# Last attention: where the two maximum tiles of a step stand between its scores and its value product

## The chip, the cores and the metric

One core of a Trainium2 chip. The metric is the device time of one execution in microseconds (us). TensorE (PE in the rows) does the matmuls, VectorE (DVE) and ScalarE (ACT) read their results out of PSUM, GpSimd (POOL) does small elementwise work, and SyncE (SP) issues the DMAs. Each engine runs its own list of instructions in order, and they meet at semaphores.

## The reference

Two gated layers over `x` of 4 batches x 1024 tokens x 256 channels: cross attention, a feed-forward mixture, cross attention again, and at the end a self attention in place of the second feed-forward. Only the last one matters here:

```python
qkv = (x @ W_qkv).reshape(Bx, Nx, 3, H, D)            # 16 heads of 16
...
pos = sim > 0.9
logits = jnp.einsum('bqhd,bkhd->bhqk', q * scale, k)
def masked_attn(tok_mask):
    ...
    a = jax.nn.softmax(l, axis=-1)
    return jnp.einsum('bhqk,bkhd->bqhd', a, v)
```

Each token attends within its own class (positive or negative), and the first five, the registers, to both.

## The kernel before

The last attention is cut into 16 units (`UNITS`), each 4 heads of one batch. A unit has 16 steps `s`: two halves of 512 queries, and in each half 8 blocks of 128 keys. A step makes, for its 4 heads, the scores of 128 keys by 512 queries, their exponentials, and the product with the values. Softmax needs each query's maximum before the scores are exponentiated: it is found one unit ahead, from a cheaper form of the scores, and enters the real scores as one more row of the contraction (row 98, `MAX_ROW`).

TensorE's list in the steady part is `body_pe`. Its pieces are:

- `scores2(u, s, h, j)`, L1607 to L1614: the scores of one head, four matmuls of 99 rows x 32 columns x 512 (L1612), one for each 32 keys, side by side on the four column groups. The result goes to one of three PSUM banks, 4 to 6, taken in turn (`take_third`, in the order of the list `USERS`). Score n can be written only once the user three places before it has been read.
- `values2(u, s, j)`, L1597 to L1605: the value product of one step, float32, four matmuls of 128 rows x 32 columns x 512 which the trace shows as two passes of four (L1603).
- `max_tile(p, a, j)`, L1584 to L1592: a maximum tile, two matmuls of 50 rows x 128 columns x 512 (L1590), on rows 0 and 64 of the array. It takes a pair of banks, 0 and 1 or 2 and 3, by turns (`take_pair`): tile p waits until VectorE has reduced tile p - 2 (`s_tfree`).
- `max_rows(o, half)`, L1594: a transpose (L1595) of the maxima of 16 tiles, into one of the three small banks.

In the code a step issues scores 0, 1 and 2, the value product of the step before, score 3, and then `turns(plan[2n])` and `turns(plan[2n + 1])`, which are its two maximum tiles. I call them A and B. `PLAN` holds one tile per slot, and in slots 2 and 18 the transposition (`("rows", ...)`) ahead of the tile. So one step in eight has a transposition, between score 3 and tile A. Units 0 to 14 have tiles: 15 x 16 = 240 steps with two tiles, 30 of them with a transposition. Unit 15 has none (`PLAN_LAST` keeps one transposition), and parts of the final projection take their place.

VectorE reduces each tile over 1024 columns (L2140, `reduce_tile`) and negates the transposed rows into `mro` (L2144, `rows_turn`), in the order of `PLAN` (`body_dve`). ScalarE exponentiates the scores of each step from the small banks to SBUF (L1083, `exps`); twice a unit it copies bank 7 of finished outputs out (L1090), ahead of its fourth exponential of that step. SyncE writes `mro` to DRAM and reads it back as the row 98 of the queries (`store_row`, L644 to L649), and loads the operands of units ahead. Its row for half 1 is read from step 8 of the same unit on, and the one for half 0 from step 0 of the next unit.

Of the kernel before, what the change touches and what calls it, by code (L numbers as in the profile page):

```python
# [38 lines left out]
def build_program(nc, ins, out):  # L39
    ctx = ExitStack()  # L40
    with ctx:
# [26 lines left out]
        def bank(i, n=1):  # L68
            return ps[:, 512 * i:512 * (i + n)]
# [372 lines left out]


        PLAN = [[("tile", n)] for n in range(32)]
        PLAN[2].insert(0, ("rows", 1))
        PLAN[18].insert(0, ("rows", 0))
        PLAN_LAST = [[] for _ in range(32)]
        PLAN_LAST[2].append(("rows", 1))
        PAIRS0 = 33
        TURNS = sum(len(x) for x in PLAN)  # L450

# [3 lines left out]
        def small_turn(u, what, arg):  # L455
            return 2 * u + SMALL.index((what, arg))
# [656 lines left out]
        def _(pe):  # L1113
# [54 lines left out]
            for b in range(B):  # L1168
# [5 lines left out]
                for g in range(4):  # L1174
                    n = 4 * b + g
# [401 lines left out]
            def take_third(what, n):  # L1577
                place = PLACE[what, n]
                if place >= 3:
                    before, i = USERS[place - 3]  # L1580
                    pe.wait_ge(s_sfree if before == "score" else s_bfree, i + 1)
                return third_bank(what, n)

            def max_tile(p, a, j):  # L1584

                pl = take_pair(p)
                q, h = a // 4, a % 4
                for i in range(2):
                    v = slice(64 * i, 64 * i + MROWS)
                    mm = pe.matmul(pl[:, 512 * i:512 * i + 512], QMH[j][h][v, P * q:P * q + P], KM[j][v, h, :],  # L1590
                                   start=True, stop=True)
                mm.then_inc(s_turn, 1)  # L1592

            def max_rows(o, half):  # L1594
                pe.transpose(o[0:16, 0:P], MX[:, half].rearrange("p j q -> p (j q)"), identF[:, :]).then_inc(s_turn, 1)  # L1595

            def values2(u, s, j):  # L1597
                half, k = s // 8, s % 8
                pe.wait_ge(s_sfree, 64 * u + 4 * s + 4)
                if k == 0:  # L1600
                    pe.wait_ge(s_oe2, 2 * u + half + 1)
                for h in range(4):
                    mm = pe.matmul(bank(7)[32 * h:32 * h + 32, :], VST[j][:, k, h, :], PR[:, s % 2, h, :],  # L1603
                                   start=(k == 0), stop=(k == TB - 1))
                mm.then_inc(s_pv2, 1)  # L1605

            def scores2(u, s, h, j):  # L1607
                n = 4 * s + h
                o = take_third("score", 64 * u + n)
                for c in range(4):  # L1610
                    t = P * (s % 8) + 32 * c
                    mm = pe.matmul(o[32 * c:32 * c + 32, :], KST[j][0:MAX_ROW + 1, h, t:t + 32],  # L1612
                                   QST[j][0:MAX_ROW + 1, h, 512 * (s // 8):512 * (s // 8) + 512],
                                   start=True, stop=True)  # L1614
                mm.then_inc(s_sco, 1)

            def body_pe(u, j, loads, last=False):
                jn = 1 - j
                p = PAIRS0 + 32 * u

                def turns(entries):
                    for what, arg in entries:
                        if what == "tile":
                            max_tile(p + arg, arg, jn)
                        else:
                            o = take_third("small", small_turn(u, what, arg))
                            pe.wait_ge(s_tfree, p + 16 * (1 - arg))
                            max_rows(o, arg)

                if not last:  # L1630
                    pe.wait_ge(s_mst[jn], 16 * MSTACK_DMAS * loads)
                plan = PLAN_LAST if last else PLAN
                for n, s in enumerate(ORDER):

                    us, js = (u, j) if s >= SHIFT else (u + 1, jn)
                    if s < SHIFT and last:
                        break
                    if s == 8:
                        pe.wait_ge(s_row[1], 16 * (u + 1))
                    if s == 0:  # L1640
                        pe.wait_ge(s_stk[jn], 16 * STACK2_DMAS * loads)
                        pe.wait_ge(s_row[0], 16 * (u + 2))
                    for h in range(3):
                        scores2(us, s, h, js)
                    if s == 0:
                        values2(u, 15, j)
                    else:
                        if s == 1:
                            pe.wait_ge(s_vst, u + 2)
                        values2(us, s - 1, js)  # L1650
                    scores2(us, s, 3, js)
                    turns(plan[2 * n])
                    turns(plan[2 * n + 1])
                    if last:
                        project2(n)
                if last:
                    values2(u, 15, j)

            def project2(i):
                c, q = i // 4, i % 4  # L1660
                n = NC + c
                if i == 0:
                    pe.wait_ge(s_tfree, PAIRS0 + 32 * (UNITS - 1))
                    pe.wait_ge(s_avg, 2)
                if i == 4 * (NC - 2):
                    pe.wait_ge(s_avg, 4)
                if i == 4 * (NC - 1):
                    pe.wait_ge(s_nd2, UNITS)
                if q == 0 and c >= 2:
                    pe.wait_ge(s_x3, n - 1)  # L1670
                o = bank(2 * (c % 2) + q // 2)[:, C * (q % 2):C * (q % 2) + C]
                for j in range(2):
                    mm = pe.matmul(o, OT2[:, j, c // 2, 512 * (c % 2) + P * q:512 * (c % 2) + P * q + P],  # L1673
                                   wproj[:, j, :], start=(q % 2 == 0 and j == 0), stop=(j == 1),
                                   skip_group_check=True)
                if q == 3:
                    mm.then_inc(s_wo, 1)
# [3 lines left out]
            n = 0  # L1681
# [31 lines left out]
            for u in range(UNITS):  # L1713
                body_pe(u, u % 2, (u + 1) // 2 + 1, last=u + 1 == UNITS)
# [542 lines left out]
```

## Time and profile before

| | us |
|---|---|
| median of 3 runs | 1285.85 (1282.24 to 1290.98) |
| the profiled execution | 1284.64 |
| its span, first to last instruction | 1282.9 |
| PE, DVE, ACT busy in the span | 1183.9, 985.4, 827.1 |

The span leaves out 1.7 us of the profiled execution. A row of the timeline merges neighbouring instructions of one line on one engine: its start is that of the first, its second number is the time from there to the end of the last. In the rows PE is a matmul and PEld a load of its weights, which may run beside an earlier matmul. The end of a matmul is modelled, and it runs past the start of the next: so the distance between two starts says what a matmul costs, not its length.

### The profile page before, as it was taken

Reading aid. Unit: us, or ns where it says so; the run is one execution under the profiler, and the core shown is the slowest. Engines: PE = TensorE matmul, PEld = TensorE weight load, DVE = VectorE, ACT = ScalarE, POOL = GpSimd, SP = SyncE. Lnnn points to the kernel's source line nnn. Section 1 sums busy time; section 2 is a strip of 40 time slices with the busy share of each in tenths; the row PEclk is TensorE's granted clock in tenths of the full one; section 3 lists DMA queues with packets and bytes.
Section 4 is the critical chain, followed back from the end, with each engine's and each line's share of the span. In section 5 each row is a group of like instructions: output and inputs, shape, how many; then the busy total and the mean of one; then the engine's idle time right before and its main releaser. Section 6 shows DMA issues by size and latency. Waiting matters only on the chain.

```text
span 1282.9 us, 26149 instructions
## 1 busy us (share of the span) xinstructions
PE 1183.9 (92%) x10378; PEld 543.5 (42%) x10378; DVE 985.4 (77%) x1446; ACT 827.1 (64%) x1476; POOL 247.9 (19%) x192
## 2 busy tenths in 40 slices
PE   4888992999999899987999999999999999999997
PEld 3566772555548446443332323233232332323345
DVE  4895597565545757657999999999999999999912
ACT  1224583677762463212888888888888888888872
POOL 2130224455661332370000000000000000000000
PEclk8879995999999999988999999999999999999999
DMA  6100016666520143453154534554345443554014
GB/s 196 27 1 15 2 25 113 118 131 113 104 51 1 50 147 111 142 75 52 45 99 82 74 86 77 95 93 80 80 88 93 82 84 76 99 94 80 11 41 137
DMA packets 89961, 101.73 MB, mean 79 GB/s; under 512 B 22122, under 2 KB 60268, under 8 KB 89840
## 3 DMA queue, kind: packets, MB, share of 16 engines
q1 hardware_dynamic: 89840, 100.06, 38.4%
q8 instruction: 83, 1.36, 0.5%
q14 instruction: 38, 0.31, 0.1%
HBM read 71.47 MB, written 24.33 MB: 75 GB/s over the span
## 4 chain that ended last, share of the span: by engine, by line
PE 60%; DVE 31%; ACT 3%; issue 2%; DMA 2%; SPq 1%; POOL 1%; POOLq 0%; DVEq 0%; ACTq 0%
DVE sm L2140 23%; PE ps L1612 10%; PE ps L1603 9%; PE ps L1590 7%; PE ps L1473 3%; PE ps L1379 2%; PE ps L1370 2%; PE ps L1371 2%; PE ps L1673 2%; PE ps L1432 2%; PE ps L1337 1%; PE ps L1335 1%; PE ps L1388 1%; PE ps L1481 1%; PE ps L1260 1%
## 5 line engine op out<-in xcount | busy, mean ns | idle before, releaser
L2140 DVE TENSOR_REDUCE sm<-ps 128x1 f32<-128x1024 f32 x512 | 602.0, 1218 | 35.2 <-PE ps L1590 31.2
L1083 ACT ACTIVATE W<-ps 128x512 f32<-128x512 f32 x1024 | 535.1, 604 | 124.4 <-PE ps L1612 122.0
L1612 PE MATMUL ps<-R 99*32 99x512 bf16 x4096 | 317.7, 384 | 0.9
L1603 PE MATMUL ps<-W,R 128*32 128x512 f32 x2048 | 266.1, 595 | 0.0
L1612 PEld LDWEIGHTS ps<-R 99*32 99x32 bf16 x4096 | 85.3, 94 | 203.8 <-ACT W L1083 156.6
L1590 PE MATMUL ps<-R 50*128 50x512 bf16 x512 | 90.7, 389 | 13.5 <-DVE sm L2140 9.1
L1590 PE MATMUL ps<-KM,R 50*128 50x512 bf16 x512 | 88.7, 384 | 5.2 <-DVE sm L2140 0.2
L1006 ACT ACTIVATE R<-ps 77x512 f32<-77x512 f32 x128 | 75.1, 592 | 23.9 <-PE ps L1371 14.4
L851 POOL COPY R<-R 128x512 f32<-128x512 f32 x16 | 9.7, 611 | 387.2 <-PE ps L1603 387.2
L1603 PEld LDWEIGHTS ps<-W,R 128*32 128x32 f32 x2048 | 63.1, 111 | 46.0 <-issue 1.0
L1918 DVE TENSOR_REDUCE small<-ps 128x4 bf16<-128x308 f32 x128 | 57.5, 473 | 23.1 <-PE ps L1337 22.9
L794 POOL COPY R<-R 4x2048 bf16<-4x2048 bf16 x32 | 60.5, 1890 | 60.0 <-ACT R L988 54.0
L1590 PEld LDWEIGHTS ps<-R 50*128 50x128 bf16 x512 | 23.2, 93 | 99.8 <-issue 58.2
L1590 PEld LDWEIGHTS ps<-KM,R 50*128 50x128 bf16 x512 | 23.3, 93 | 95.9 <-issue 64.9
L870 POOL TENSOR_TENSOR R<-R,W 128x512 f32<-128x512 f32 x8 | 10.2, 1273 | 270.2 <-DMA W<-sum_factors 270.2
L1473 PE MATMUL ps<-R,W 128*128 128x512 f32 x128 | 57.9, 595 | 0.0
L1749 DVE TENSOR_SCALAR XN<-X,mv,rstd 128x256 f32<-128x256 f32 x128 | 46.7, 433 | 9.7 <-PE ps L1149 9.5
L1370 PE MATMUL ps<-R 100*77 100x512 bf16 x128 | 49.0, 383 | 0.0
L1371 PE MATMUL ps<-R 77*77 77x512 bf16 x128 | 48.6, 380 | 0.0
L1937 DVE RECIPROCAL small<-ps 128x16 f32<-128x16 f32 x32 | 8.2, 258 | 47.1 <-PE ps L1388 47.1
L1335 PE MATMUL ps<-R 77*128 77x308 bf16 x128 | 38.6, 302 | 3.8 <-DMA R<-x_parts 3.7
L1337 PEld LDWEIGHTS ps<-R 96*128 96x128 bf16 x512 | 35.0, 99 | 12.9
(258 smaller groups left out, 1505.3 us busy)
## 6 DMA issues: line engine op xcount, KB each, us to landing
R<-x_parts SPq DMA_DIRECT2D x96, 128.0 KB, 4.8
R<-q_parts SPq DMA_DIRECT2D x192, 64.0 KB
R<-q_parts SPq DMA_DIRECT2D x96, 128.0 KB
R<-k_parts SPq DMA_DIRECT2D x96, 128.0 KB
x_parts<-R SPq DMA_DIRECT2D x8, 768.0 KB, 6.5
q_parts<-R SPq DMA_DIRECT2D x24, 256.0 KB, 2.6
k_parts<-R SPq DMA_DIRECT2D x24, 256.0 KB, 2.7
X<-in_x SPq DMA_DIRECT2D x4, 1024.0 KB, 10.0
```

The lines of the kernel that those rows point to most:

```text
L794: pool.tensor_copy(Xs[m // 2 % 3][SR:SR1, :, 512 * (m % 2):512 * (m % 2) + 512], mrow1[:, m % 2].unsqueeze(1).to_broadcast([4, 4, 512])).t ...
L1006: act.activation(P1[:, m % 2, j, :], score_bank1(n)[0:KX, :], ACT.Exp, scale=0.25).then_inc(s_e1, 1)
L1083: act.activation(PR[:, s % 2, h, :], third_bank("score", 64 * u + n), ACT.Exp, scale=0.25).then_inc(s_sfree, 1)
L1335: pe.matmul(o, mb1[:, P * q:P * q + P], I4, start=True, stop=False, skip_group_check=True)
L1370: pe.matmul(o, K1s[:, 4 * hg + j, KX * b:KX * b + KX], Xs[u % 3][:, j, t], start=True, stop=False)
L1371: pe.matmul(o, I4[:, 0:KX], mb1[:, t], start=False, stop=True).then_inc(s_sc, 1)
L1473: mm = pe.matmul(o[:, 512 * j:512 * j + 512], wqkv[:, i, C * kind + P * j:C * kind + P * j + P], XNT3[:, i, 512 * c:512 * c + 512], start= ...
L1590: mm = pe.matmul(pl[:, 512 * i:512 * i + 512], QMH[j][h][v, P * q:P * q + P], KM[j][v, h, :], start=True, stop=True)
L1603: mm = pe.matmul(bank(7)[32 * h:32 * h + 32, :], VST[j][:, k, h, :], PR[:, s % 2, h, :], start=(k == 0), stop=(k == TB - 1))
L1612: mm = pe.matmul(o[32 * c:32 * c + 32, :], KST[j][0:MAX_ROW + 1, h, t:t + 32], QST[j][0:MAX_ROW + 1, h, 512 * (s // 8):512 * (s // 8) + 51 ...
L1918: dve.tensor_reduce(Mn[:, u % 2, q, :], bank(n % 2)[:, 0:4 * KX].rearrange("p (j n) -> p j n", j=4), AX, ALU.max, negate=True).then_inc(s_ ...
L2140: dve.tensor_reduce(MX[:, half, h, q:q + 1], bank(2 * ((p + 1) % 2), 2), AX, ALU.max).then_inc(s_tfree, 1)
```

## The change

In `body_pe`, tile A moves ahead of score 3, directly behind the value product. Tile B stays behind score 3. The transposition moves from the slot of tile A to that of tile B, in the plan of TensorE, VectorE and the bank order alike, so that it still follows score 3 and the order of `USERS` is what it was.

```diff
         PLAN = [[("tile", n)] for n in range(32)]
-        PLAN[2].insert(0, ("rows", 1))
-        PLAN[18].insert(0, ("rows", 0))
+        PLAN[3].insert(0, ("rows", 1))
+        PLAN[19].insert(0, ("rows", 0))
         PLAN_LAST = [[] for _ in range(32)]
-        PLAN_LAST[2].append(("rows", 1))
+        PLAN_LAST[3].append(("rows", 1))
...
                         values2(us, s - 1, js)
+                    turns(plan[2 * n])
                     scores2(us, s, 3, js)
-                    turns(plan[2 * n])
                     turns(plan[2 * n + 1])
```

A step of TensorE was: score 0, 1, 2, value product, score 3, (transposition), A, B. It becomes: score 0, 1, 2, value product, A, score 3, (transposition), B. VectorE's order in a step with a transposition was: rows, A, B. It becomes: A, rows, B.

## Rows read from the trace of the kernel before

**Rows 1.** The page: busy time of each engine, and its 40 slices

```profile
PE 1183.9 (92%) x10378; PEld 543.5 (42%) x10378; DVE 985.4 (77%) x1446; ACT 827.1 (64%) x1476; POOL 247.9 (19%) x192
...
PE   4888992999999899987999999999999999999997
...
DVE  4895597565545757657999999999999999999912
ACT  1224583677762463212888888888888888888872
...
PEclk8879995999999999988999999999999999999999
```

**Rows 2.** Groups of instructions by line, between 640 and 1200 us

```profile
L1612 PE MATMUL ps<-R 99*32 99x512 bf16 x3520 | 270.9, 382 | 0.8
...
L1595 PE MATMUL ps<-identF,sm 128*16 128x128 f32 x27 | 7.5, 277 | 0.0
```

**Rows 3.** Who waited for whom, 640 to 1220 us: total, times, longest

```profile
PEld ps L1590 <- DVE sm L2140: 43.0, 114, 0.6
DVE sm L2140 <- PE ps L1590: 25.5, 86, 0.4
```

**Rows 4.** Timeline of PE, three steps from 813.26 us: start, us

```profile
813.26 0.83 PE L1612 MATMUL ps<-R 99*32 99x512 bf16 x12
813.92 1.03 PE L1603 MATMUL ps<-W,R 128*32 128x512 f32 x8
814.78 0.39 PE L1612 MATMUL ps<-R 99*32 99x512 bf16 x4
815.10 0.28 PE L1595 MATMUL ps<-identF,sm 128*16 128x128 f32 x1
815.31 0.61 PE L1590 MATMUL ps<-R 50*128 50x512 bf16 x4
815.85 0.83 PE L1612 MATMUL ps<-R 99*32 99x512 bf16 x12
816.51 1.03 PE L1603 MATMUL ps<-W,R 128*32 128x512 f32 x8
817.37 0.39 PE L1612 MATMUL ps<-R 99*32 99x512 bf16 x4
817.69 0.86 PE L1590 MATMUL ps<-R 50*128 50x512 bf16 x4
818.48 0.83 PE L1612 MATMUL ps<-R 99*32 99x512 bf16 x12
...
820.00 0.39 PE L1612 MATMUL ps<-R 99*32 99x512 bf16 x4
820.32 0.60 PE L1590 MATMUL ps<-R 50*128 50x512 bf16 x4
820.86 0.83 PE L1612 MATMUL ps<-R 99*32 99x512 bf16 x12
```

**Rows 5.** Timeline of the weight loads (PEld) from 817.01 us

```profile
817.01 0.10 PEld L1612 LDWEIGHTS ps<-R 99*32 99x32 bf16 x4 [0.38 <-ACT W L1083]
817.68 0.10 PEld L1590 LDWEIGHTS ps<-R 50*128 50x128 bf16 x2 [0.57 <-issue]
818.15 0.10 PEld L1590 LDWEIGHTS ps<-R 50*128 50x128 bf16 x2 [0.37 <-DVE sm L2140]
```

**Rows 6.** Timeline of DVE, 810 to 822 us

```profile
810.53 4.74 DVE L2140 TENSOR_REDUCE sm<-ps 128x1 f32<-128x1024 f32 x4 [0.33 <-PE ps L1590]
815.42 0.28 DVE L2144 TENSOR_SCALAR XN<-ps 16x128 bf16<-16x128 f32 x1 [0.15 <-PE ps L1595]
...
820.75 2.36 DVE L2140 TENSOR_REDUCE sm<-ps 128x1 f32<-128x1024 f32 x2 [0.27 <-PE ps L1590]
```

**Rows 7.** Timeline of all engines, near 810 us and from 815.7 us

```profile
809.43 1.38 ACT L1083 ACTIVATE W<-ps 128x512 f32<-128x512 f32 x2
809.78 0.39 PE L1612 MATMUL ps<-R 99*32 99x512 bf16 x4
...
815.74 2.36 DVE L2140 TENSOR_REDUCE sm<-ps 128x1 f32<-128x1024 f32 x2
...
816.36 1.58 ACT L1083 ACTIVATE W<-ps 128x512 f32<-128x512 f32 x3 [0.52 <-PE ps L1612]
```

**Rows 8.** Timeline of PE at 446 us: float32 of 32 columns, then 128 columns

```profile
446.01 0.59 PE L1473 MATMUL ps<-R,W 128*128 128x512 f32 x1
446.44 0.60 PE L1467 MATMUL ps<-identF,W 128*128 128x128 f32 x4
...
447.44 0.60 PE L1458 MATMUL ps<-R,sm 128*32 128x512 f32 x2
447.97 0.33 PE L1445 MATMUL ps<-identF,XN 128*128 128x128 f32 x1
```

**Rows 9.** SyncE's queue from 815.72 us: the maxima's way through DRAM

```profile
815.72 0.32 SPq L646 DMA_DIRECT2D max_rows<-XN  x1
820.36 0.62 SPq L648 DMA_DIRECT2D R<-max_rows  x1
821.35 6.68 SPq L590 DMA_DIRECT2D R<-q_parts  x12
```

## The prediction

> **What bounds the kernel now.** I read the page first: PE is busy for 92% of the span, at full clock (9 tenths and more) in the second half, where the change lies, and DVE for 77% [rows 1]. Two engines near their limit call for a look at single steps. The groups by line count them: 3520 matmuls of L1612 between 640 and 1200 us, 16 a step, so 220 steps in 560 us, 2.545 us each, and 27 transpositions, about one in eight steps [rows 2]. The 240 steps with tiles take 240 x 2.545 = 610.8 us.
>
> The timeline of PE shows three kinds of step [rows 4]. The one from 813.26 to 815.85 us has a transposition and takes 2.59 us; the next takes 2.63 us, the one after it 2.38 us (818.48 to 820.86). The last two differ behind score 3 only: its two tiles and the way back to score 0 take 0.79 us (817.69 to 818.48) or 0.54 us (820.32 to 820.86). The weight loads say why: that of tile B starts at 818.15 us, released by the reduction L2140 [rows 5], which ran from 815.74 to 818.10 us [rows 7]. So a semaphore takes 0.05 us, and B waits for the pair of banks that the tile two before it held. The waits count 114 of these in 580 us, about every second step; DVE in turn waited 86 times for a tile [rows 3]. Four reductions run in one piece of 4.74 us, then DVE idles some 0.3 us [rows 6]. So TensorE alone needs 2.38 us for a plain step, VectorE 4.74 / 2 = 2.37 us, and they miss each other because both tiles are asked for together. That is the waste that an order with A and B apart can take away: 2.63 - 2.38 = 0.25 us in every second step.
>
> **The change part by part.** No instruction is added or removed, only the order. Per step on TensorE, by distances of starts:
>
> - Scores 0 to 2: 0.66 us (815.85 to 816.51), 0.22 us each. The value product to the next score: 0.86 us (816.51 to 817.37) [rows 4]. Unchanged.
> - A score followed by a tile takes 0.32 us (817.37 to 817.69, and 820.00 to 820.32), 0.10 us more than one followed by a score [rows 4]. The load of a score's weights comes 0.36 us before its matmul (817.01 against 817.37), but a tile's behind a score comes with it (817.68 against 817.69), although its banks can be long free [rows 4, 5]. A tile followed by a score takes 0.33 us (load 818.15, next score 818.48) [rows 4, 5]; of the pair at 820.32 us that leaves 0.54 - 0.32 = 0.22 us for a tile followed by a tile. So a change between the two shapes of array (50 rows x 128 columns, 99 x 32) costs 0.10 us each way, and the present step pays it twice.
> - After the change the step changes shape four times: value product to A, A to score 3, score 3 to B, B to score 0. Three of these are in the rows. The first is not. Its lower bound is nothing (0.86 us stays), the upper the same 0.10 us. The nearest rows are float32 of 32 columns followed by 128 columns, 0.53 us (447.44 to 447.97), where a float32 pass followed by its own shape takes 0.43 us (446.01 to 446.44) [rows 8]. I take 0.10 us. The sum for a plain step is 0.66 + 0.96 + 0.32 + 0.33 + 0.32 = 2.59 us; the 0.33 gives score 3 a hundredth, since its weights aren't loaded ahead either.
>
> The Trainium skill (TensorEngine Tiling (Array Packing), Key Properties) speaks against this change: changing the tiling mode, not just the tile, drains the TensorE. It covers the pair that the rows lack, since the value product is in the mode of four column tiles and the maximum tile in that of two row tiles. By it the plain step stays at 2.59 us; without a drain there it would be 2.49 us.
>
> Does anything wait in that step? VectorE: A starts it 0.43 us after its own start (820.32 to 820.75 us), and A and B take 2.36 us [rows 4, 6], so B's reduction has released its banks at 0.43 + 2.36 + 0.05 = 2.84 us behind A. The next B comes at 2.59 + 0.32 + 0.33 = 3.24 us. The 114 waits go, and VectorE idles 0.23 us a step instead. Next late is TensorE itself, in its order.
>
> ScalarE: score 2 of the next step takes the bank of score 3. Score 3 starts its exponential 0.43 us later when ScalarE is idle (809.78 us; the second of two that end at 810.81 us and take 0.60 us each, thus 810.21) [rows 7]. With 0.60 us for it and 0.05 us the bank is free 1.08 us behind score 3. TensorE gets there in 0.33 + 0.32 + 0.22 + 0.22 = 1.09 us, where it has 0.32 + 0.54 + 0.44 = 1.30 us now. I price it at nothing, but the cover is one hundredth: each hundredth that is missing costs 240 x 0.01 = 2.4 us. Below nothing it can't be, as nothing waits there in the plain step. In the 30 steps with a copy of bank 7 (twice a unit) the fourth exponential comes later: a step's exponentials start 0.51 us behind score 0 (815.85 to 816.36) and 0.49 us apart [rows 4, 7], so with a copy between them it starts at 0.51 + 4 x 0.49 = 2.47 us, against 1.94 + 0.43 = 2.37 us. Some 0.08 us in 30 steps: 2.4 us.
>
> **The steps with a transposition.** Now it costs little: 2.59 us in place of 2.505 us (the mean of 2.63 and 2.38), because it falls into the wait for B. After the change nothing waits, so it counts in full: score 3 to transposition 0.32 us, on to B 0.21 us (815.10 to 815.31) [rows 4], against 0.33 us; 0.20 us more. And VectorE now does A ahead of the rows. They leave PSUM at 0.43 + 1.14 (2.36 less the 1.22 of the second reduction) + 0.28 + 0.05 = 1.90 us behind A, or 1.98 us if nothing overlaps [rows 6, 7]. Three places behind the rows in the turn of small banks stands score 2 of the next step. TensorE is there after 0.32 + 0.33 + 0.21 + 0.32 + 0.22 + 0.22 = 1.62 us. It waits 0.28 to 0.36 us, and all that TensorE has is behind it: I take 0.33 us. Step: 2.59 + 0.20 + 0.33 = 3.12 us.
>
> The rows reach SyncE's queue about 1 us later than now: 0.66 + 0.96 + 0.43 + 1.14 = 3.19 us behind the step's start, against 2.16 us (813.26 to 815.42) [rows 4, 6]. Their read-back is issued 4.6 us behind the store (815.72, 820.36) [rows 9] and is due at step 8, five steps of 2.59 us behind: hidden. So is what queues behind it, loads for a unit ahead. GpSimd waits only for value products of whole units. In unit 15 there are no tiles, and the transposition stands where it stood: nothing.
>
> **The sum.** 210 x 2.59 + 30 x 3.12 + 2.4 = 543.9 + 93.6 + 2.4 = 639.9 us, against 610.8 us: 29.1 us slower. The profiled execution took 1284.64 us, the median 1285.85 us; from the median it comes to 1315 us.
>
> **The rivals.**
>
> - *Changing shape is free once loads aren't asked for in a bunch.* The two tiles' wait is the whole loss, and 0.10 us is only bad luck of the order. The TensorE step would be 2.59 - 0.42 = 2.17 us, VectorE would bound with 2.37 us, 2.37 + 0.32 us where it copies rows: 210 x 2.37 + 30 x 2.69 = 578.4 us, 32 us faster, 1253 us. It decides from where the two new changes cost under 0.09 us together, since 610.8 less the transpositions' 30 x 0.53 and 2.4 us leaves 2.47 us a step. Against it: the 0.32 and 0.33 us stand there with and without a wait [rows 4, 5]. Chance 0.03. The Trainium skill (TensorE: Matmul & The Clock Gate, Step-by-step: what each phase is for) would let it be so: loads are pulled ahead of running matmuls when they go to the background weight buffer. The trace agrees for scores alone.
> - *The value product lets A in for nothing.* 2.49 us by TensorE; the exponential's loop is then 1.08 + 0.22 + 0.86 + 0.32 = 2.48 us, about the same. 210 x 2.50 + 30 x 3.02 + 2.4 = 618 us: 7 us slower, 1293 us. For it: this pair is in no row. Chance 0.06.
> - *The transposition's bank isn't waited for* (0.33 x 30 = 10 us less): 1305 us. Against it is the order in VectorE's list. Chance 0.08.
> - *The exponential of score 3 becomes the bound.* If its loop is 0.05 us longer than I add up, each step has that: 12 us more, 1327 us. For it: the cover is one hundredth, and each of the terms on both sides is read to a hundredth only. Chance 0.09.
>
> That the order isn't what the code says can be left out: each engine runs its list in order.
>
> **How the numbers follow.** The forecast holds 0.74. Range 1303 to 1327 us: it takes in the third rival and the near half of the fourth, and leaves out the first two. A measurement of this kernel tells about 1% from no change. Faster by over 1%: 0.03, the first rival. Within 1%: 0.06, the second. Slower: 0.91.
>
> **What would show it.** Right: in the timeline every plain step takes 2.59 to 2.60 us, no more alternation; value product to L1590 takes 0.96 us, L1590 to L1612 0.32 us; in the waits the 114 of L1590 for DVE are gone, DVE waits for L1590 over 200 times, some 0.2 us each; in the steps after a transposition score 2 waits some 0.3 us for L2144. Wrong: plain steps at 2.37 us with DVE in one piece (first rival), 0.86 us from value product to tile (second), or score 2 waiting for ScalarE in plain steps (fourth).

## The result: 2.6% slower, and the profile after

The changed kernel takes 1318.62 us (median of 4 runs, 1316.13 to 1324.23), the kernel before 1287.15 us in the same comparison. The ratio on record is 1.0262, with a 95% interval of 1.0221 to 1.0302 (the two medians alone give 1.0244). The forecast was 1315 us in a range of 1303 to 1327. The profiled execution took 1316.13 us, 31.5 us more than the 1284.64 us of before.

The page of the changed kernel, first its busy times, as in [rows 1], and then the chain that ended last, which is the work that set the time, followed back from the last instruction:

```profile
PE 1226.6 (93%) x10378; PEld 532.6 (41%) x10378; DVE 983.2 (75%) x1446; ACT 849.0 (65%) x1476; POOL 248.2 (19%) x192
...
PE 81%; DVE 12%; DMA 2%; ACT 1%; issue 1%; SPq 1%; POOL 1%; POOLq 0%; DVEq 0%
```

The counts are the same: nothing but order changed. The chain of before:

```profile
PE 60%; DVE 31%; ACT 3%; issue 2%; DMA 2%; SPq 1%; POOL 1%; POOLq 0%; DVEq 0%; ACTq 0%
```

VectorE's share fell from 31% to 12%, and PE's rose from 60% to 81%; between 812 and 824 us every piece of the chain is now PE's.

Where is the time? The value product L1603 runs from the first step to the last, so its first and last starts frame the last attention. First the kernel before, then the changed one:

```profile
L1603 PE MATMUL ps<-W,R x2048: 590/594/1061, 604.3 to 1259.7; 128*32 128x512 f32 x187
```

```profile
L1603 PE MATMUL ps<-W,R x2048: 590/594/1061, 603.5 to 1289.5; 128*32 128x512 f32 x187
```

That is 655.4 us and 686.0 us: 30.6 of the 31.5 us lie between them. I use this distance below and call it the attention's length. Each is read from one trace.

Counted over both traces, the 210 plain steps took 533.7 us and now 550.4 us, and the 30 steps with a transposition 77.6 us and now 92.6 us. So the 30 make almost half of the loss.

The timeline of PE in the changed kernel, a plain step, one with a transposition and the start of the next, as in [rows 4]:

```profile
819.44 0.85 PE L1612 MATMUL ps<-R 99*32 99x512 bf16 x12
820.11 1.03 PE L1603 MATMUL ps<-W,R 128*32 128x512 f32 x8
821.08 0.39 PE L1590 MATMUL ps<-R 50*128 50x512 bf16 x2
821.40 0.40 PE L1612 MATMUL ps<-R 99*32 99x512 bf16 x4
821.73 0.39 PE L1590 MATMUL ps<-R 50*128 50x512 bf16 x2
822.05 0.85 PE L1612 MATMUL ps<-R 99*32 99x512 bf16 x12
...
823.69 0.39 PE L1590 MATMUL ps<-R 50*128 50x512 bf16 x2
824.01 0.40 PE L1612 MATMUL ps<-R 99*32 99x512 bf16 x4
824.34 0.28 PE L1595 MATMUL ps<-identF,sm 128*16 128x128 f32 x1
824.55 0.39 PE L1590 MATMUL ps<-R 50*128 50x512 bf16 x2
824.87 1.11 PE L1612 MATMUL ps<-R 99*32 99x512 bf16 x12
825.81 1.03 PE L1603 MATMUL ps<-W,R 128*32 128x512 f32 x8
```

The plain step from 819.44 to 822.05 us takes 2.61 us: 0.67 for three scores, 0.97 from the value product to tile A, then 0.32, 0.33 and 0.32 us. The plain steps don't alternate any more: 180 take 2.61 or 2.62 us, and the 30 in which ScalarE copies bank 7 take 2.67 us (816.77 to 819.44 us is one). The step from 822.05 us has a transposition and takes 2.82 us, and the three scores behind it take 0.94 us (824.87 to 825.81) in place of 0.67. The weight loads and VectorE say why:

```profile
822.50 0.10 PEld L1612 LDWEIGHTS ps<-R 99*32 99x32 bf16 x4 [0.33 <-ACT W L1083]
...
825.59 0.10 PEld L1612 LDWEIGHTS ps<-R 99*32 99x32 bf16 x4 [0.37 <-DVE XN L2144]
```

```profile
824.12 1.23 DVE L2140 TENSOR_REDUCE sm<-ps 128x1 f32<-128x1024 f32 x1 [0.26 <-PE ps L1590]
825.27 0.27 DVE L2144 TENSOR_SCALAR XN<-ps 16x128 bf16<-16x128 f32 x1
```

Score 2's load at 825.59 us waits for VectorE's negated rows, which end at 825.54 us, because the reduction of A went ahead of them. In a plain step (822.50 us) the same load is released by ScalarE. And the waits between 640 and 1220 us, against [rows 3]:

```profile
DVE sm L2140 <- PE ps L1590: 63.0, 210, 0.6
PEld ps L1590 <- DVE sm L2140: 27.9, 34, 0.8
PEld ps L1612 <- DVE XN L2144: 10.0, 27, 0.4
```

Loads of a tile waited for VectorE 114 times. VectorE is still named 34 times, but at no price where the rows show it: the load at 826.77 us, behind the transposition step, names it, and its tile starts 0.97 us behind the value product (825.81 to 826.78) like the others. VectorE waited 86 times for a tile and now 210 times. So the change did what it says: B finds its banks free. TensorE lost more by it than it got.

### The profile page after: what moved, and what is told of

Its sections match the earlier page's. It is cut to its first block, busy times and chain, and to the rows that moved or that the text cites. A ratio compares the mean times of both kernels' runs of the same rounds, so it can differ in the third digit from the quotient of the medians.

```text
span 1314.3 us, 26149 instructions
## 1 busy us (share of the span) xinstructions
PE 1226.6 (93%) x10378; PEld 532.6 (41%) x10378; DVE 983.2 (75%) x1446; ACT 849.0 (65%) x1476; POOL 248.2 (19%) x192
## 4 chain that ended last, share of the span: by engine, by line
PE 81%; DVE 12%; DMA 2%; ACT 1%; issue 1%; SPq 1%; POOL 1%; POOLq 0%; DVEq 0%
PE ps L1612 20%; PE ps L1603 17%; PE ps L1590 12%; DVE sm L2140 4%; PE ps L1473 3%; PE ps L1379 2%; PE ps L1370 2%; PE ps L1371 2%; PE ps L1673 2%; PE ps L1432 2%; PE ps L1337 1%; PE ps L1335 1%; PE ps L1388 1%; PE ps L1481 1%; PE ps L1260 1%
## 5 line engine op out<-in xcount | busy, mean ns | idle before, releaser
L2140 DVE TENSOR_REDUCE sm<-ps 128x1 f32<-128x1024 f32 x512 | 604.3, 1218 | 72.8 <-PE ps L1590 72.6
L1083 ACT ACTIVATE W<-ps 128x512 f32<-128x512 f32 x1024 | 556.3, 599 | 133.7 <-PE ps L1612 111.3
L1612 PE MATMUL ps<-R 99*32 99x512 bf16 x4096 | 329.0, 389 | 2.2
L1603 PE MATMUL ps<-W,R 128*32 128x512 f32 x2048 | 265.3, 594 | 0.0
L1590 PE MATMUL ps<-R 50*128 50x512 bf16 x512 | 100.7, 392 | 8.3 <-DVE sm L2140 8.3
L1590 PE MATMUL ps<-KM,R 50*128 50x512 bf16 x512 | 99.8, 386 | 0.0
L1918 DVE TENSOR_REDUCE small<-ps 128x4 bf16<-128x308 f32 x128 | 57.6, 473 | 22.8 <-PE ps L1337 22.6
L1603 PEld LDWEIGHTS ps<-W,R 128*32 128x32 f32 x2048 | 64.5, 110 | 21.9 <-issue 0.5
L1337 PE MATMUL ps<-R 96*128 96x77 bf16 x512 | 40.3, 202 | 0.0
```

The source lines that it names most:

```text
L1083: act.activation(PR[:, s % 2, h, :], third_bank("score", 64 * u + n), ACT.Exp, scale=0.25).then_inc(s_sfree, 1)
L1337: mm = pe.matmul(o[:, KX * j:KX * j + KX], Xs[u % 3][0:SR, j, P * q:P * q + P], K1s[0:SR, 4 * hg + j, KX * b:KX * b + KX], start=False, st ...
L1918: dve.tensor_reduce(Mn[:, u % 2, q, :], bank(n % 2)[:, 0:4 * KX].rearrange("p (j n) -> p j n", j=4), AX, ALU.max, negate=True).then_inc(s_ ...
L2140: dve.tensor_reduce(MX[:, half, h, q:q + 1], bank(2 * ((p + 1) % 2), 2), AX, ALU.max).then_inc(s_tfree, 1)
```

## The experiments

Ten kernels, in an order that follows the argument. The attention's length is from the first and last start of the value product in each trace; before has 655.4 us, the changed kernel 686.0 us.

**Tile A moved, the transposition not.** The transposition stands between the value product and A.

```diff
         PLAN[2].insert(0, ("rows", 1))
         PLAN[18].insert(0, ("rows", 0))
...
+                    turns(plan[2 * n])
                     scores2(us, s, 3, js)
-                    turns(plan[2 * n])
                     turns(plan[2 * n + 1])
```

`USERS` lists the transposition ahead of score 3 to match.

> Tile A ahead of score 3 as in the changed kernel, but the transposition stays in the slot of tile A, so it stands between the value product and A. My theory (TensorE's order bounds; four changes of shape a step; the negated rows behind a reduction cost a wait in 30 steps): plain steps of 2.61 us as in the changed kernel, transposition steps of 2.82 us, and no wait of some 0.3 us for the transposed rows behind them: about 8 us faster than the changed kernel, some 23 us slower than before (1310 us). Rival (the move of the transposition is what costs): as before, 1287 us.

Measured: 1308.64 us, ratio to before 1.0186 (1.0162 to 1.0210); length 678.2 us, 22.8 us over before and 7.8 us under the changed kernel. Its timeline of PE around a transposition:

```profile
820.55 0.60 PE L1605 MATMUL ps<-W,R 128*32 128x512 f32 x4
821.08 0.28 PE L1597 MATMUL ps<-identF,sm 128*16 128x128 f32 x1
...
822.26 0.85 PE L1614 MATMUL ps<-R 99*32 99x512 bf16 x12
822.94 1.03 PE L1605 MATMUL ps<-W,R 128*32 128x512 f32 x8
```

The scores behind the transposition take 0.68 us and not 0.94: the wait for the rows is gone, and 30 x 0.26 = 7.8 us with it. All the rest of the loss stays. Taken as the first of the two moves, the tile's makes 22.8 of the 30.6 us, as expected.

**The transposition moved, the tiles not.**

```diff
-        PLAN[2].insert(0, ("rows", 1))
-        PLAN[18].insert(0, ("rows", 0))
+        PLAN[3].insert(0, ("rows", 1))
+        PLAN[19].insert(0, ("rows", 0))
```

> Both tiles stay behind score 3, only the transposition moves between A and B. My theory: plain steps alternate between 2.63 and 2.38 us as before; in the 30 steps with a transposition score 2 of the next step waits 0.6 us or more for the rows, since VectorE reduces A first and TensorE is there 0.3 us sooner than in the changed kernel; one change of shape more, part of it given back as the next B finds its banks free. Sum 15 to 22 us slower than before, so that the prices of the two parts don't add up to the 31 us of both. Rival (the tile's move is all that costs): as before, 1287 us.

Measured: 1305.19 us, ratio 1.0150 (1.0126 to 1.0173); length 674.8 us, 19.4 us over before. The timeline of PE:

```profile
826.25 0.28 PE L1595 MATMUL ps<-identF,sm 128*16 128x128 f32 x1
...
826.78 0.61 PE L1612 MATMUL ps<-R 99*32 99x512 bf16 x8
827.82 0.40 PE L1612 MATMUL ps<-R 99*32 99x512 bf16 x4 [0.43 <-DVE XN L2144]
```

Score 2 starts 1.04 us behind score 0 in place of 0.44: it waits 0.60 us for the rows, more than the 0.26 us of the changed kernel, since here TensorE comes to it sooner. The parts alone cost 22.8 and 19.4 us, together 30.6 us. They aren't additive. For the wait for the rows the traces show why: it is 0.60 us alone and 0.26 us where A stands ahead of score 3.

**Half of the reductions' work left out,** in the kernel before and in the changed one. Half of the maxima is left out with it.

```diff
-                dve.tensor_reduce(MX[:, half, h, q:q + 1], bank(2 * ((p + 1) % 2), 2), AX, ALU.max)
+                dve.tensor_reduce(MX[:, half, h, q:q + 1], bank(2 * ((p + 1) % 2)), AX, ALU.max)
```

> The kernel before, but each reduction reads 512 of its tile's 1024 columns (so half of the maxima is left out). My theory: B's wait is VectorE's time, so it goes: plain steps of 2.38 us without alternation, 22 to 26 us faster than before. Rival (the alternation is made by ScalarE or by loads of weights): no change.

> The changed kernel with reductions of 512 of 1024 columns. My theory: TensorE's own order bounds there, so plain steps stay at 2.61 us; only the wait for the transposed rows goes (30 x 0.27 us): 7 to 9 us faster than the changed kernel, still over 20 us slower than before. Rival (VectorE's waits are still what bounds): 25 us faster or more.

A reduction takes 0.69 us in these kernels in place of 1.22 us. Measured: 1245.64 us from before, 41 us faster, one run; length 628.1 us, 27.3 us less, against 22 to 26 us expected. The stretch ahead of the first value product, in which the tiles of the first unit stand, gave another 11.5 us (it starts at 592.8 us, not 604.3), which I hadn't counted. Not all of that is the reductions' own time: between 592 and 604 us the granted clock was 1.00 in this run and 0.76 before. From the changed kernel: 1299.53 us, one run; length 678.4 us, 7.6 us less, and 7.2 us ahead of it. So "7 to 9 us faster" holds for the length alone. The whole kernel became 19 us faster than the changed one and is 13 us slower than before, where I had expected over 20. Timelines of PE, before with half reductions and then changed with half reductions:

```profile
815.87 0.83 PE L1612 MATMUL ps<-R 99*32 99x512 bf16 x12
...
818.25 0.83 PE L1612 MATMUL ps<-R 99*32 99x512 bf16 x12
```

```profile
815.46 0.86 PE L1612 MATMUL ps<-R 99*32 99x512 bf16 x12
...
818.08 0.85 PE L1612 MATMUL ps<-R 99*32 99x512 bf16 x12
```

Before, 179 of the 210 plain steps take 2.37 or 2.38 us now: the alternation was VectorE's. One takes 2.48 us, and the other 30 take 2.69 us, with half reductions and without. They are the ones in which ScalarE copies bank 7: one runs from 805.84 to 808.53 us in the first of these traces, and its three scores take 0.97 us in place of 0.66. So those 30 are bound by ScalarE's list. In the changed kernel the plain step (815.46 to 818.08) stays at 2.62 us with VectorE's work about halved. VectorE doesn't bound there: the same cut gives 27.3 us in the one order and 7.6 us in the other, and those 7.6 us are the wait for the transposed rows.

**Eight narrow matmuls a tile,** in the changed kernel, the columns cut as for the scores.

```diff
-                    mm = pe.matmul(pl[:, 512 * i:512 * i + 512], QMH[j][h][v, P * q:P * q + P], KM[j][v, h, :],
+                    for c in range(4):
+                        mm = pe.matmul(pl[32 * c:32 * c + 32, 512 * i:512 * i + 512],
+                                       QMH[j][h][v, P * q + 32 * c:P * q + 32 * c + 32], KM[j][v, h, :],
```

> The changed kernel, but each half of a maximum tile is four matmuls of 50 rows x 32 columns in place of one of 50 x 128: the columns of the array are cut as for the scores, the rows still differ (50 against 99). If any change of shape costs 0.10 us, plain steps stay at 2.61 us. If only a change of the columns costs, they fall to VectorE's 2.37 to 2.40 us and the kernel is faster than before (1255 to 1265 us). If the two halves no longer run side by side, a tile takes 0.43 us in place of 0.22 us: 3.0 us a step.

Measured: 1326.05 us, one run; length 692.3 us. Its timeline of PE:

```profile
814.65 0.83 PE L1614 MATMUL ps<-R 99*32 99x512 bf16 x12
815.31 1.03 PE L1605 MATMUL ps<-W,R 128*32 128x512 f32 x8
816.28 0.41 PE L1591 MATMUL ps<-KM,R 50*32 50x512 bf16 x8
816.62 0.40 PE L1614 MATMUL ps<-R 99*32 99x512 bf16 x4
816.95 0.41 PE L1591 MATMUL ps<-KM,R 50*32 50x512 bf16 x8
```

Value product to tile is still 0.97 us, and from a tile to the score behind it 0.34 us: the eight matmuls run side by side, and the plain step takes 2.63 us, forecast 2.61. The columns alone are not what costs, or the steps would have fallen to 2.40 us.

**The same with rows 0 to 49 alone, and then with the scores' own shape,** both in the changed kernel. In the first both halves take rows 0 to 49 (the keys of one half twice). In the second all operands are the identity matrix, 99 rows of it, so its maxima aren't those of the scores.

```diff
-                                       QMH[j][h][v, P * q + 32 * c:P * q + 32 * c + 32], KM[j][v, h, :],
+                                       QMH[j][h][0:MROWS, P * q + 32 * c:P * q + 32 * c + 32], KM[j][0:MROWS, h, :],
```

And the second, against the first:

```diff
-                                       QMH[j][h][0:MROWS, P * q + 32 * c:P * q + 32 * c + 32], KM[j][0:MROWS, h, :],
+                                       identB[0:MAX_ROW + 1, 32 * c:32 * c + 32],
+                                       identB[0:MAX_ROW + 1, :].unsqueeze(1).to_broadcast([MAX_ROW + 1, 4, P]),
```

> The changed kernel, each half of a maximum tile made by four matmuls of rows 0 to 49 x 32 columns (the second half gets the keys of the first, so half of the maxima is of other keys). The two halves share rows and so follow each other: 0.43 us a tile in place of 0.22 us. If 50 rows against 99 is a change of shape, value product to tile stays at 0.53 us (second pass) and a plain step takes 2.61 + 2 x 0.21 = 3.03 us. If only rows 64 and up in use make the change, a second pass goes to the tile in 0.43 us and the four changes vanish: 0.66 + 0.86 + 0.43 + 0.22 + 0.43 = 2.60 us a step, about the changed kernel's time.

> As e9, eight matmuls a tile, but each of 99 rows x 32 columns x 512, the scores' own shape. They read the identity matrix and not the queries and keys, so the maxima are not those of the scores (left out). My theory (a change of shape costs, nothing else about a tile does): the second pass of the value product goes to the tile in 0.43 us in place of 0.53, the tile to score 3 in 0.43 us (two times 0.216) with no 0.10 us on top, score 3 to the tile in 0.22 us: 0.66 + 0.86 + 0.43 + 0.22 + 0.43 = 2.60 us a plain step, 0.43 us less than in e9 (3.03 us) with the same number and length of matmuls; in all within 10 us of the changed kernel, some 100 us faster than e9. Rival (a tile costs its 0.10 us whatever its shape, by its wait for VectorE or its place in the list): 3.0 us a step as e9.

Measured: 1417.27 us and 1319.45 us, one run each; length 779.9 and 688.6 us. Timelines of PE, 50 rows and then 99 rows:

```profile
812.86 0.40 PE L1614 MATMUL ps<-R 99*32 99x512 bf16 x4
813.19 0.61 PE L1591 MATMUL ps<-KM,R 50*32 50x512 bf16 x8
813.74 0.83 PE L1614 MATMUL ps<-R 99*32 99x512 bf16 x12
814.39 1.03 PE L1605 MATMUL ps<-W,R 128*32 128x512 f32 x8
815.36 0.61 PE L1591 MATMUL ps<-KM,R 50*32 50x512 bf16 x8
```

```profile
815.83 1.03 PE L1606 MATMUL ps<-W,R 128*32 128x512 f32 x8
816.69 0.60 PE L1591 MATMUL ps<-identB 99*32 99x512 bf16 x8
817.12 0.39 PE L1615 MATMUL ps<-R 99*32 99x512 bf16 x4
817.34 0.60 PE L1591 MATMUL ps<-identB 99*32 99x512 bf16 x8
```

These two have eight matmuls a tile in two groups, in the same place. They differ in the rows and in what the tiles read. With 50 rows it is 0.97 us from value product to tile, 0.33 us from score to tile, 0.55 us from tile to score. With 99 rows it is 0.86, 0.22 and 0.43 us. Each of the four changes of shape costs 0.10 to 0.12 us, and the plain step takes 3.04 and 2.61 us, forecast 3.03 and 2.60. That it is the rows and not the identity matrix shows in the scores: they read real operands with 99 rows in every kernel, and follow each other in 0.22 us. This pair is the clearest evidence for the term that the prediction rested on.

**Both tiles ahead of score 3.**

```diff
+                    turns(plan[2 * n])
+                    turns(plan[2 * n + 1])
                     scores2(us, s, 3, js)
-                    turns(plan[2 * n])
-                    turns(plan[2 * n + 1])
```

This is against the kernel before; the transposition goes ahead of score 3 with its tile, and `USERS` lists it so.

> Both tiles and the transposition between the value product and score 3: two changes of shape a step as before, no tile behind score 3. My theory: score 2 of the next step needs the bank of score 3, 1.09 us behind it, and TensorE is there after 0.22 x 3 = 0.66 us, so the exponential of score 3 bounds: 1.09 + 0.22 + 0.96 + 0.54 = 2.81 to 2.83 us a plain step, some 70 us slower than before (1355 to 1362 us), with score 2 waiting 0.44 us for ScalarE in every step. Rival (only changes of shape cost): 2.38 to 2.50 us a step, not slower than before.

Measured: 1359.21 us, one run; length 728.2 us, 72.8 us over before. The timeline of PE:

```profile
812.58 0.83 PE L1614 MATMUL ps<-R 99*32 99x512 bf16 x12
813.68 0.40 PE L1614 MATMUL ps<-R 99*32 99x512 bf16 x4 [0.27 <-ACT W L1085]
813.91 1.03 PE L1605 MATMUL ps<-W,R 128*32 128x512 f32 x8
...
815.41 0.83 PE L1614 MATMUL ps<-R 99*32 99x512 bf16 x12
```

The piece of 12 is score 3, 0 and 1; score 2 waits until 813.68 us, 1.10 us behind score 3, for the exponential that frees score 3's bank. The step takes 2.83 us. It has only two changes of shape, as before, and is the slowest order of all: the loop by score 3's bank is real. Priced at 1.08 us, it takes 1.10 us.

**Tile A ahead in the even positions alone,** those in which B waits in the kernel before.

```diff
+                    if n % 2 == 0:
+                        turns(plan[2 * n])
                     scores2(us, s, 3, js)
-                    turns(plan[2 * n])
+                    if n % 2:
+                        turns(plan[2 * n])
                     turns(plan[2 * n + 1])
```

> Tile A ahead of score 3 in the even positions of a unit alone, those in which B waits 0.25 us before; the odd ones, the transpositions among them, as before. My theory: the two more changes of shape (0.21 us) take the place of the wait (0.25 us), so that TensorE spends about the same: within 5 us of before. Rival (separating the tiles frees VectorE, which then bounds at 2.37 us a step): 30 us faster. Rival (moving A costs more than its changes of shape): 15 us slower, half of the whole change.

Measured: 1285.11 us, ratio 1.0001 (0.9986 to 1.0015); length 654.2 us. The timeline of PE:

```profile
813.44 0.83 PE L1612 MATMUL ps<-R 99*32 99x512 bf16 x12
814.10 1.03 PE L1603 MATMUL ps<-W,R 128*32 128x512 f32 x8
815.06 0.39 PE L1590 MATMUL ps<-R 50*128 50x512 bf16 x2
815.38 0.40 PE L1612 MATMUL ps<-R 99*32 99x512 bf16 x4
815.75 0.39 PE L1590 MATMUL ps<-R 50*128 50x512 bf16 x2
816.07 0.83 PE L1612 MATMUL ps<-R 99*32 99x512 bf16 x12
```

The even step is again 2.63 us: two changes of shape, and 0.04 us of wait left (0.37 us from score 3 to B, not 0.33). The wait of 0.25 us and the two changes have about the same price, and where one takes the other's place nothing is won.

**ScalarE's copy of bank 7 behind its fourth exponential,** in the kernel before.

```diff
-                    if h == 3:
-                        between()
...
+                between()
```

> The kernel before, with ScalarE's copy of bank 7 behind the fourth exponential of its step in place of ahead of it (30 steps). In the trace of before score 2 of the step behind waits 0.05 us for ScalarE after such a copy, or 0.3 us. My theory of the exponential's loop (the bank of score 3 is asked for 1.30 us behind it): those waits go, and the value product that waits for the copy gets up to 0.1 us in their place: 1 to 4 us faster than before, so at most 0.3%. Rival (the copy's place is off TensorE's path): no change at all, the waits of 0.05 and 0.3 us stay.

Measured: 1284.94 us against 1285.68, ratio 0.9986 (0.9972 to 1.0000); length 652.8 us, 2.6 us less than before. The traces agree with the size expected: the 30 plain steps with the copy take 2.54 to 2.63 us and not 2.69, some steps beside them more, and all 210 together 2.5 us less. But the timed difference can't be told from none. It is the only order with a median below that of before, and I don't claim it as a gain.

## Why the prediction was right

*What bounds.* Right: with half reductions the alternation of before went, to 2.38 us, and the changed kernel's plain step didn't move. Not seen: the 30 plain steps with the copy of bank 7 take 2.69 us before, bound by ScalarE and not by VectorE, and the sum counts them on the side of before only through the mean of 2.545 us.

*Shape changes.* The plain step came out at 2.61 us, forecast 2.59. The term without a row, value product to tile, was taken at 0.96 us and measured 0.97. The second rival, with no price there, falls with it. The first wanted VectorE to bound at 2.37 us, and it falls too. The Trainium skill (TensorEngine Tiling (Array Packing), Key Properties) says that changing the tiling mode, and not just the tile, drains the TensorE. The trace agrees that a change costs, 0.10 to 0.12 us each between 50 and 99 rows. Whether those 0.10 us are a drain isn't shown. The load of a tile's weights takes 0.10 us and starts only with its matmul (817.68 and 817.69 us in [rows 4, 5]), and no run tells the two apart.

*ScalarE's loop.* It was priced at nothing with a cover of 0.01 us, and the cover wasn't there. In each plain step score 2's load is released by ScalarE, 1.10 us behind the start of score 3 (821.40 to 822.50) and not 1.08, and the three scores take 0.67 to 0.68 us, not 0.66. Where TensorE comes there a little later, in the kernel of narrow tiles, they take 0.66 us (814.65 to 815.31), and with half reductions still 0.68 us (815.46 to 816.14): the wait is ScalarE's. The fourth rival happened, with 0.02 us in place of its 0.05. With rounding in the other terms this is the 0.02 us by which the step was missed: 210 x 0.02 = 4 us. The steps with a copy of bank 7 were given 0.08 us each and took 0.06 us, 1.7 us in all where the sum has 2.4.

*The transposition.* The step and the wait behind it were taken at 3.12 us and measured 2.82 + 0.27 = 3.09 us. The wait is 0.26 to 0.27 us, just below the 0.28 to 0.36 us given: VectorE freed the bank 1.90 us behind A (A's start is 823.69 us, score 2's load 825.59), the lower end of what I had worked out, and I had leaned to the upper. That returned 1 us.

*The sum.* 29.1 us forecast, 30.6 us in the attention. It is nearer than its parts: the 240 steps lost 31.7 us (643.0 less 611.3), and 1.1 us came back outside them, which the forecast left out. Of that, 0.7 us is the distance between the first two value products (2.99 us before, 2.31 now; the granted clock between 600 and 608 us was 0.50 before, the lower level of 1.2 GHz throughout, and 0.68 now, at 2.4 GHz for a part), and the rest the wait of the first piece of the final projection. That part is luck. The remaining 0.9 us of the difference between the profiled executions lies ahead of and behind the attention, where nothing was changed; I have no cause for it.

*What was not said.* That the two parts overlap. One alone costs 22.8 us, the other 19.4 us, and both 30.6 us.

## What to carry to other kernels

Price an order of instructions by the distances of starts between each pair of kinds, since the price of a matmul depends on what stood before it. Separating two instructions that wait for the same consumer takes the wait away, but if a matmul of another shape comes between them the changes of shape can cost more than the wait did. An instruction that "costs nothing" beside a wait costs in full once the wait is gone, and so does its place in the consumer's order.

## What the runs showed of the hardware that I had not expected

Matmuls of 50 rows x 32 columns beside ones of 99 rows x 32 columns pay the change of shape as much as those of 50 x 128 (0.97 us from value product to tile in both): rows alone suffice, even where all are in rows 0 to 49. But not every difference in rows costs. Float32 passes of 128 rows and bfloat16 matmuls of 99 rows, both of 32 columns, follow each other at no price: 0.22 us from score to value product, and 0.86 us for its two passes before a tile of the scores' shape, as before a score.
